# A two-layer graph network on one core: the rarely taken rounds of layer one move out of the loop, and unread products are added to it

## The chip, the core and the metric

The kernel runs on one core of one Trainium2 chip. The core has five engines that run side by side and meet at semaphores: TensorE (PE: matrix products; its weight loads are shown as PEld), VectorE (DVE), ScalarE (ACT), GpSimd (POOL, which here issues the gathering DMAs) and SyncE (SP, which issues the plain DMAs). The metric is the time of one execution on the device in microseconds. The kernel before takes 2933.87 us (median of 3 runs, 2928.56 to 2934.1).

## The reference

There are 6250 nodes with 64 features each and 200000 edges, each with a source, a target and (for layer one) a weight; the edges are sorted by target. Cut to what matters:

```python
h = maximum(layernorm(x), 0)
# layer one
m = edge_weight[:, None] * (h @ W + b)[src]
agg = segment_sum(m, dst) / (segment_sum(edge_weight, dst)[:, None] + 1e-6)
x = x + relu(agg)
h = maximum(layernorm(x), 0)
# layer two
m = gelu(concat(h[src], edge_attr) @ W_msg + b_msg)
agg = segment_sum(m, dst)
x = x + gelu(((1 + eps) * h + agg) @ W_upd + b_upd)
```

## The kernel before, in words

The 200000 edges are cut into 196 groups of 1024 edges, and four groups (numbered s = 0 to 3) make a body, so that both layers have 49 bodies. Since the edges are sorted by target, the targets of a group mostly lie within a window of 72 nodes. A group's sum by target is a product of its edges' rows with a one-hot matrix of target places (`onehots`, L1373; the product is `window`, L989), which VectorE adds to the sums of all nodes (`sums`, L1463, then a small `tick`, L1483).

**Layer one** gets the source rows of a group in two ways. Some tiles of 128 edges (3 or 4 of 8) are gathered by GpSimd from a table. The other tiles (`JA` of them, 5 or 4) are not gathered: VectorE makes one-hot matrices of their sources and targets (`tile_onehots`, L1379 and L1381; all of a group by `build`), TensorE multiplies them into a small adjacency block (`blocks_of`, L927), ScalarE copies the block out (L720), and once per body TensorE multiplies the whole adjacency with the table (`adjacency_sums`, 98 products of L946). That result is copied (L734), turned back (`sums_back`, L957 and L958) and copied by VectorE (`rows_of_sums`, L1420) to stand beside the gathered rows.

The bodies of layer one run in stretches that `STRETCHES` sets: bodies 0 to 13 are a loop (the first stretch, 5 tiles of 5 columns), 14 and 15 stand as straight code, 16 to 46 are a loop again (the second stretch, 4 tiles of 10 columns), and 47 and 48 stand as straight code. In the function `first` one body works one ahead: TensorE makes the blocks of body b + 1 while it sums body b, and VectorE builds the one-hots of groups 2 and 3 of body b + 1 and of groups 0 and 1 of body b + 2. The order on each engine is the order in which `first` is written. A ring of two groups holds the one-hots of the tiles, so `build` of a group waits until TensorE has multiplied the group two before it: `build(ahead, b + 1, 2)` waits for the tiles of `blocks_of(ahead, b + 1, 0)`.

Targets that do not fit a tile's 5 or 10 columns need **further rounds** (`further_rounds`). They stand at the head of every body on TensorE and VectorE: a flag of the body (`more_flags`) is loaded, and a conditional block follows that is passed over where the flag is not set. The block holds a whole round for all tiles: on VectorE a loop with three or four instructions for each of the 16 or 20 tiles, on TensorE all their products. In this execution no body enters it: the trace has no instruction of the lines inside it, such as L1503 or L1522. TensorE's loops in layer one are emitted with a hint for the jump back (`hint_back_edge`), VectorE's without.

**Layer two** (`second`) is another loop over 48 bodies and a straight last one. It picks two of eight tiles by products with the whole table (L917), gathers the others, multiplies the edges' features (L1115) and sums with windows as before.

`busy(n)` issues n products of 192 columns (L1018) into a bank of PSUM that nobody reads. Before the change it stands in the last body of layer one, between the layers and at the end of layer two.

## Time and profile before

| what | value |
|---|---|
| median of 3 runs | 2933.87 us |
| the profiled execution, its own time | 2940.75 us |
| its span, first to last instruction | 2938.9 us |
| TensorE busy / VectorE busy | 89% / 71% |
| granted clock of TensorE over the span | 0.947 |
| layer one's bodies | about 104 to 1350 us |
| layer two's bodies | about 1400 to 2908 us |

The profiled execution took 1.9 us more than its span, and 6.9 us (0.2%) more than the median of the runs. In the rows below, a timeline row gives an instruction's start, its duration, its engine and line, what it writes and reads, and in square brackets how long its engine had been idle before it and who ended that; "issue" means that the engine waited for nothing that the profile shows. Several instructions of one kind in a row are merged into one row with their count.

### The profile page before, as it was taken

How to read it: one execution, taken by the hardware profiler on the slowest of the kernel's cores; microseconds unless marked ns; L12 is line 12 of the kernel's file. 1: busy time of each engine (PE TensorE's matmuls, PEld its weight loads, DVE VectorE, ACT ScalarE, POOL GpSimd, SP SyncE). 2: the span in 40 equal slices, each digit the busy share in tenths (PEclk: the TensorE clock that was granted, in tenths of full speed). 3: DMA queues.
4: the chain of work that ended last, by engine and by line, in shares of the span. 5: the costliest groups of instructions: out<-in, count | busy, mean ns of one | idle time of the engine just before them, and what ended most of it. 6: DMA issues, size and time to landing. Idle time of an engine off the chain costs nothing.

```text
span 2938.9 us, 72786 instructions
## 1 busy us (share of the span) xinstructions
PE 2615.2 (89%) x22325; PEld 2440.5 (83%) x22326; DVE 2088.3 (71%) x4375; ACT 1617.3 (55%) x5144; POOL 1820.8 (62%) x1911
## 2 busy tenths in 40 slices
PE   1788877887888888788999999999999999999999
PEld 1678777777777777777999999999999999999998
DVE  8766667667667666766777777777777777777774
ACT  2555555455555555545556656556656565665653
POOL 3355555555555555552777777777777777777771
PEclk9999998888888888888999999999999999999997
DMA  6010111110111111111454444544444545444442
GB/s 125 16 20 19 21 21 20 22 22 20 21 22 20 21 22 21 20 21 44 109 124 119 121 121 118 121 118 121 117 120 118 123 115 123 119 119 120 118 120 45
DMA packets 473383, 216.56 MB, mean 74 GB/s; under 512 B 264997, under 2 KB 442025, under 8 KB 473077
## 3 DMA queue, kind: packets, MB, share of 16 engines
q1 hardware_dynamic: 412404, 151.55, 19.8%
q0 software_dynamic: 60672, 62.25, 11.5%
q14 instruction: 276, 2.25, 0.3%
q8 instruction: 31, 0.51, 0.1%
HBM read 208.14 MB, written 5.51 MB: 73 GB/s over the span
## 4 chain that ended last, share of the span: by engine, by line
PE 52%; DVE 0%; ACT 0%; issue 0%; DVEq 0%
PE ps L917 38%; PE ps L1115 7%; PE ps L989 4%; PE ps L1104 3%; PE ps L1062 1%; PE ps L1018 0%; DVE rows L1446 0%; DVE parts L1211 0%; DVE sel L1442 0%; DVE room L1635 0%; ACT h_sb L847 0%; DVE h_sb L1666 0%; DVE h_sb L1671 0%; ACT h_sb L865 0%; DVE tick L1483 0%
## 5 line engine op out<-in xcount | busy, mean ns | idle before, releaser
L628 POOL DMA_INDIRECT rows<-p_table,idx x1176 | 1110.0, 944 | 395.5 <-issue 350.0
L917 PE MATMUL ps<-parts,pick_all 128*128 128x448 f32 x5488 | 1167.0, 369 | 2.2 <-DVE parts L1211 2.2
L917 PEld LDWEIGHTS ps<-parts,pick_all 128*128 128x128 f32 x5488 | 1017.8, 188 | 83.5 <-issue 2.6
L628 POOL DMA_INDIRECT rows<-h_table,idx x720 | 694.2, 964 | 616.1 <-ACT room L759 422.5
L720 ACT COPY adj<-ps 128x500 f32<-128x500 f32 (+1 forms) x848 | 394.8, 518 | 308.2 <-PE ps L927 298.0
L927 PE MATMUL ps<-hot_c,hot_p 128*128 128x125 f32 (+1 forms) x2336 | 470.7, 304 | 63.9 <-issue 57.3
L927 PEld LDWEIGHTS ps<-hot_c,hot_p 128*128 128x128 f32 x2336 | 393.0, 212 | 80.5 <-issue 72.2
L1442 DVE TENSOR_TENSOR sel<-ps,mask 128x896 f32<-128x896 f32 x196 | 214.0, 1092 | 310.1 <-PE ps L917 302.0
L1425 DVE TENSOR_SCALAR pick_all<-src_all,node_f 128x1792 fp32r<-128x1792 int16 x196 | 406.6, 2075 | 28.6 <-issue 26.2
L989 PE MATMUL ps<-onehot,room 128*65 128x72 f32 (+1 forms) x3400 | 227.0, 237 | 193.7 <-DVE onehot L1373 98.2
L989 PEld LDWEIGHTS ps<-onehot,room 128*65 128x65 f32 (+1 forms) x3400 | 197.7, 144 | 228.2 <-issue 118.2
L946 PE MATMUL ps<-adj,h_sb 128*64 128x160 f32 (+1 forms) x4802 | 352.7, 312 | 8.9 <-issue 7.9
L1373 DVE TENSOR_TENSOR onehot<-iota,dw 128x360 f32<-128x360 f32 (+1 forms) x196 | 99.4, 507 | 357.8 <-issue 354.2
L946 PEld LDWEIGHTS ps<-adj,h_sb 128*64 128x64 f32 x4802 | 340.8, 152 | 14.8 <-issue 12.4
L1446 DVE TENSOR_REDUCE rows<-sel 128x128 f32<-128x896 f32 x196 | 342.8, 1749 | 6.7
L1381 DVE TENSOR_SCALAR hot_c<-iota_c,scal 128x250 fp32r<-128x250 f32 (+1 forms) x848 | 325.8, 384 | 0.0
L1379 DVE TENSOR_SCALAR hot_p<-iota_p,scal 128x256 fp32r<-128x256 f32 (+1 forms) x848 | 309.6, 365 | 20.8 <-PE ps L927 20.5
L927 PE MATMUL ps<-hot_lo,hot_p 128*128 128x250 f32 x1056 | 285.2, 304 | 0.0
L847 ACT ACTIVATE h_sb<-room 128x512 f32<-128x512 f32 x98 | 62.0, 632 | 356.0 <-DVE room L1635 356.0
L927 PEld LDWEIGHTS ps<-hot_lo,hot_p 128*128 128x128 f32 x1056 | 230.3, 218 | 0.0
L1115 PE MATMUL ps<-W1b_sb,eT 128*128 128x128 f32 x1568 | 216.6, 281 | 0.0
L1381 DVE TENSOR_SCALAR hot_lo<-iota_c,scal 128x250 fp32r<-128x250 f32 x528 | 213.4, 404 | 0.0
(180 smaller groups left out, 2592.4 us busy)
## 6 DMA issues: line engine op xcount, KB each, us to landing
src_all<-keys SPq DMA_DIRECT2D x196, 448.0 KB
ea<-in_edge_attr_dram SPq DMA_DIRECT2D x196, 256.0 KB
rows<-p_table,idx POOLq DMA_INDIRECT x1176
rows<-h_table,idx POOLq DMA_INDIRECT x720
x_sb<-in_x_dram SPq DMA_DIRECT2D x6, 224.0 KB, 4.0
h_table<-h_sb SPq DMA_DIRECT2D x6, 224.0 KB
p_table<-h_sb SPq DMA_DIRECT2D x6, 224.0 KB
out_dram<-h_sb SPq DMA_DIRECT2D x6, 224.0 KB
```

Source lines behind the costliest of these rows:

```text
L628: nc.gpsimd.indirect_dma_start(out=rows[:, s, j, 0:D], out_offset=None, in_=table[:, :], in_offset=bass.IndirectOffsetOnAxis(ap=idx[:, s, ...
L720: nc.scalar.copy(adj[:, :, t * z.WT:(t + 1) * z.WT], psA[t % BANKS1][:, 0:KH * KW * z.WT].rearrange("p (k w) -> p k w", w=z.WT)).then_inc( ...
L917: last = nc.tensor.matmul(to, hot[:, k, t * P:(t + 1) * P], parts[:, part, k, :, :].rearrange("p a d -> p (a d)"), start=(k == 0 and part ...
L927: last = nc.tensor.matmul(to[:, k * KW * z.WT:(k + 1) * KW * z.WT], one[:, k * P:(k + 1) * P], two[i], start=(i == 0), stop=(i == z.WP - 1))
L946: last = nc.tensor.matmul(psX[h:h + D, 0:z.cols], h_sb[:, n, :], adj[:, n, 0:z.cols], start=(n < 2), stop=(n >= NB - 2))
L989: last = nc.tensor.matmul(psW[s % 2][at:at + width, :], lhs(j), hot[:, j, :], start=(j < sets), stop=(j >= n - sets))
L1115: last = nc.tensor.matmul(psM[:, q * P:(q + 1) * P], eT[:, q * P:(q + 1) * P], W1b_sb[:, :], start=True, stop=True)
L1379: nc.vector.tensor_scalar(one, iota_p[:, :], number(0), None, ALU.is_equal)
L1381: last = nc.vector.tensor_scalar(two[i], iota_c[:, 0:KW * z.WT], number(1), number(2 + i), ALU.is_equal, ALU.mult)
L1425: nc.vector.tensor_scalar(pick_all[:, q % 2, :].rearrange("p (k e) -> p k e", k=KA), src_bc[:, q % 2, :, 0:PICKS * P], node_f[:, 0:1], Non ...
L1442: nc.vector.tensor_tensor(sel[:, :, :, :], ps[:, bank:bank + PICKS, 0:NA * D].rearrange("p t (a d) -> p t a d", d=D), of.unsqueeze(3).to_b ...
L1446: nc.vector.tensor_reduce(rows[:, q % SLOTS, J0:J, 0:D], sel[:, :, :, :].rearrange("p t a d -> p t d a"), AX.X, ALU.add).then_inc(s_prow, 1)
```

## The change

Two things change in layer one. First, the further rounds of all bodies stand in one block (`all_rounds`) at the head of the last body, on TensorE and on VectorE. It is entered only where a new flag `row_any` (the maximum of the bodies' flags, one more VectorE instruction before the loops) is set, and then runs over all bodies. The loops and the other straight bodies hold no such block any more. Second, `busy(10, psX[:, 0:IDLE])` stands ahead of each pair of windows, for the 48 bodies that have one after them: two times ten products of 192 columns in each body, written into the bank of the adjacency sums, which the next `adjacency_sums` starts anew.

```diff
+        row_any = sb("row_any", [1, 1], i32)
...
-            def further_rounds(z, b, more):
-
-                with pe.If((more & (1 << SLOTS)) > 0):
+            def further_rounds(z, b):
+
+                with pe.If((more_flags(b) & (1 << SLOTS)) > 0):
                     count = pe.value_load(row_b[0:1, bass.ds(b, 1), 0], min_val=1, max_val=N)
                     before = pe.value_load(row_b[0:1, bass.ds(b, 1), 1], min_val=0, max_val=N * BODIES)
-                    pe.wait_ge(s_sumTc, b + 2)
-                    pe.sem_inc(s_passed, 1)
                     with pe.Fori(0, count) as i:
...
-            def busy(n):
+            def busy(n, to=psG):
 
                 for _ in range(n):
-                    nc.tensor.matmul(psG, idle[:, 0:P], idle[:, 0:IDLE], start=True, stop=True)
+                    nc.tensor.matmul(to, idle[:, 0:P], idle[:, 0:IDLE], start=True, stop=True)
...
+            def all_rounds():
+
+                with pe.If(pe.value_load(row_any[0:1, 0:1], min_val=0, max_val=1) > 0):
+                    pe.wait_ge(s_sumTc, BODIES + 1)
+                    for z in ZONES:
+                        with pe.Fori(z.first, z.end) as b:
+                            further_rounds(z, b)
+
             def first(b, here, ahead, further):
                 more = more_flags(b)
-                further_rounds(here, b, more)
+                if not ahead:
+                    all_rounds()
                 if ahead:
                     blocks_of(ahead, b + 1, 0)
                 sums_back(here, b)
@@
                         blocks_of(ahead, b + 1, s)
                     if s == 1:
                         pe.wait_ge(s_sumc, b + 2)
+                    if ahead:
+                        busy(10, psX[:, 0:IDLE])
                     for r in (s - 1, s):
...
+            meta(nc.vector.tensor_reduce(row_any[:, :], row_r[:, 2, :], AX.X, ALU.max))
...
+            def all_rounds():
+
+                with dve.If(dve.value_load(row_any[0:1, 0:1], min_val=0, max_val=1) > 0):
+                    for z in ZONES:
+                        with dve.Fori(z.first, z.end) as b:
+                            further_rounds(z, b)
...
             def first(b, here, ahead, further):
                 more = more_flags(b)
-                further_rounds(here, b, more)
+                if not ahead:
+                    all_rounds()
                 for s in range(SLOTS):
                     dve.wait_ge(s_dw[0], b * SLOTS + (s + 1))
                     onehots(0, s, s_oh[0], here)
```

VectorE at the head of the second stretch's loop, before: the flag of the body (`row_i`) is loaded, and the conditional jump on line 1487 leads over the block of further rounds, whose first rows these are.

```order
L1451 TENSOR_LOAD row_i
L1451 ISA x2
L1487 REGISTER_ALU
L1487 COMPARE_AND_BRANCH
L1488 ISA
L1488 TENSOR_LOAD row_b
L1488 ISA x2
L1489 ISA
L1489 TENSOR_LOAD row_b
L1489 ISA x2
L1490 UNCONDITIONAL_BRANCH
```

The block ends some 190 rows further down with the jump on line 1487, behind which the one-hots of group 0 stand:

```order
L1490 COMPARE_AND_BRANCH
L1487 UNCONDITIONAL_BRANCH
L1560 REGISTER_ALU
L1373 TENSOR_TENSOR onehot<-iota,dw 128x360
L1387 ISA
L1391 ISA
L1379 TENSOR_SCALAR hot_p<-iota_p,scal 128x256
L1381 TENSOR_SCALAR hot_c<-iota_c,scal 128x250
```

The same place on VectorE now (lines are those of the changed kernel, some 11 to 19 higher):

```order
L1602 ISA
L1462 TENSOR_LOAD row_i
L1462 ISA x2
L1579 REGISTER_ALU
L1384 TENSOR_TENSOR onehot<-iota,dw 128x360
L1398 ISA
L1402 ISA
L1390 TENSOR_SCALAR hot_p<-iota_p,scal 128x256
L1392 TENSOR_SCALAR hot_c<-iota_c,scal 128x250
```

The load of the flag is now followed by the one-hots of group 0 at once. The whole loop has 184 rows where it had 382.

TensorE in the second stretch's loop, ahead of the windows of groups 2 and 3, before (last block of group 3, then the windows):

```order
L927 MATMUL ps<-hot_c,hot_p 128x250
L927 MATMUL ps<-hot_lo,hot_p 128x250
L995 REGISTER_ALU
L989 MATMUL ps<-onehot,room 65x72 x5
L995 REGISTER_ALU
L989 MATMUL ps<-onehot,room 65x72 x5
```

And now:

```order
L928 MATMUL ps<-hot_c,hot_p 128x250
L928 MATMUL ps<-hot_lo,hot_p 128x250
L1017 MATMUL ps<-ident 128x192 x10
L994 REGISTER_ALU
L988 MATMUL ps<-onehot,room 65x72 x5
L994 REGISTER_ALU
L988 MATMUL ps<-onehot,room 65x72 x5
```

Ten products of the identity stand between the last block and the first of the two windows. Nothing is moved on ScalarE, GpSimd or SyncE.

## Rows read from the trace of the kernel before

**Rows 1.** The page: TensorE's granted clock in 40 slices of the span, in tenths

```profile
PEclk9999998888888888888999999999999999999997
```

**Rows 2.** Windows: length, busy PE, PEld, DVE, ACT, POOL; clock, DMA share, GB/s

```profile
104.50:389.00 284.50, 238.21 (x2940) 225.11 (x2941) 183.13 (x714) 160.81 (x637) 151.37 (x157) 0.96 0.10 20
495.00:1288.00 793.00, 640.54 (x6314) 611.20 (x6313) 541.37 (x1829) 408.60 (x1421) 448.48 (x467) 0.87 0.11 21
1375.00:2900.00 1525.00, 1519.01 (x10975) 1396.44 (x10976) 1137.02 (x1191) 917.70 (x2663) 1112.98 (x1177) 0.99 0.48 117
```

**Rows 3.** Waits, 495 to 1288 us: total us, times, longest

```profile
DVE onehot L1373 <- issue: 242.1, 59, 8.2
```

**Rows 4.** Timeline of VectorE, one body of the second stretch

```profile
706.50 0.06 DVE L1483 MEMSET tick<- 1x1 f32 x1
714.12 0.53 DVE L1373 TENSOR_TENSOR onehot<-iota,dw 128x360 f32<-128x360 f32 x1 [7.56 <-issue]
714.57 0.43 DVE L1379 TENSOR_SCALAR hot_p<-iota_p,scal 128x256 fp32r<-128x256 f32 x1
...
728.91 0.52 DVE L1373 TENSOR_TENSOR onehot<-iota,dw 128x360 f32<-128x360 f32 x1
...
733.91 0.06 DVE L1483 MEMSET tick<- 1x1 f32 x1
```

**Rows 5.** Timeline of TensorE, the same body

```profile
703.09 8.65 PE L946 MATMUL ps<-adj,h_sb 128*64 128x160 f32 x98 [0.17 <-issue]
...
716.55 0.27 PE L927 MATMUL ps<-hot_lo,hot_p 128*128 128x250 f32 x1
718.92 0.81 PE L989 MATMUL ps<-onehot,room 128*65 128x72 f32 x10 [2.10 <-DVE room L1420]
720.43 1.17 PE L989 MATMUL ps<-onehot,room 128*65 128x72 f32 x10 [0.70 <-DVE onehot L1373]
...
729.48 0.84 PE L989 MATMUL ps<-onehot,room 128*65 128x72 f32 x10 [2.15 <-DVE onehot L1373]
```

**Rows 6.** Timeline of VectorE at the heads of the straight bodies 14 and 47

```profile
411.22 0.46 DVE L1373 TENSOR_TENSOR onehot<-iota,dw 128x288 f32<-128x288 f32 x1 [3.60 <-issue]
...
1310.02 0.53 DVE L1373 TENSOR_TENSOR onehot<-iota,dw 128x360 f32<-128x360 f32 x1 [2.81 <-issue]
```

**Rows 7.** Timeline of VectorE at the jump back of layer two's loop

```profile
1804.91 2.08 DVE L1425 TENSOR_SCALAR pick_all<-src_all,node_f 128x1792 fp32r<-128x1792 int16 x1 [0.55 <-issue]
```

**Rows 8.** Timeline of VectorE at the heads of bodies 1, 13, 17 and 46

```profile
128.40 0.46 DVE L1373 TENSOR_TENSOR onehot<-iota,dw 128x288 f32<-128x288 f32 x1 [6.47 <-issue]
...
392.34 0.46 DVE L1373 TENSOR_TENSOR onehot<-iota,dw 128x288 f32<-128x288 f32 x1 [6.85 <-issue]
...
495.21 0.53 DVE L1373 TENSOR_TENSOR onehot<-iota,dw 128x360 f32<-128x360 f32 x1 [8.16 <-issue]
...
1287.48 0.53 DVE L1373 TENSOR_TENSOR onehot<-iota,dw 128x360 f32<-128x360 f32 x1 [7.53 <-issue]
```

**Rows 9.** Timeline of TensorE, body 16

```profile
467.14 0.35 PE L927 MATMUL ps<-hot_c,hot_p 128*128 128x250 f32 x1 [3.24 <-issue]
...
483.78 6.98 PE L946 MATMUL ps<-adj,h_sb 128*64 128x160 f32 x98 [0.23 <-issue]
490.93 0.35 PE L927 MATMUL ps<-hot_c,hot_p 128*128 128x250 f32 x1 [0.18 <-issue]
```

**Rows 10.** Timeline of VectorE, body 16

```profile
467.89 0.36 DVE L1379 TENSOR_SCALAR hot_p<-iota_p,scal 128x256 fp32r<-128x256 f32 x1 [4.37 <-PE ps L927]
```

**Rows 11.** Windows, within the body of rows 5 (columns as rows 2)

```profile
704.40:707.80 3.40, 3.40 (x33) 3.40 (x32) 1.93 (x9) 0.60 (x4) 2.49 (x4) 0.60 0.14 29
```

**Rows 12.** TensorE alone (busy, clock, DMA share, GB/s), one body of the first stretch

```profile
185.70:207.50 21.80, 17.98 (x233) 1.00 0.10 20
```

**Rows 13.** Timeline of TensorE between the layers

```profile
1352.74 1.49 PE L1018 MATMUL ps<-ident 128*128 128x192 bf16 x16
1354.07 0.36 PE L1062 MATMUL ps<-W_sb,sums_sb 65*128 65x65 f32 x2
```

More of the change, by code:

```diff
@@ L1483, in sums, with further_rounds @@
                 nc.vector.memset(tick[:, s:s + 1], 0.0).then_inc(s_done, 1)
-            def further_rounds(z, b, more):
-                with dve.If((more & (1 << SLOTS)) > 0):
+            def all_rounds():
[3 more added lines that the diff above has]
+                            further_rounds(z, b)
+            def further_rounds(z, b):
+                with dve.If((more_flags(b) & (1 << SLOTS)) > 0):
                     count = dve.value_load(row_b[0:1, bass.ds(b, 1), 0], min_val=1, max_val=N)
```

## The prediction, made blind

> **What bounds the kernel now.** I began with the page's row of the granted clock: it is lower in the first half of the span than in the second [rows 1]. Split by stage [rows 2], layer two has TensorE busy for 1519.01 of 1525 us at a clock of 0.99: it is bound there, and the change touches nothing in it. Layer one is another case: in the second stretch TensorE is busy for 640.54 of 793 us at a clock of 0.87, VectorE for 541.37. Neither is full, so something makes them take turns.
>
> The list of waits names it: VectorE stood for 242.1 us ahead of the one-hots of line 1373, for nothing that the profile shows [rows 3]. The timeline of one body shows where. VectorE ends a body with the tick at 706.50, and its first instruction of the next starts at 714.12, 7.56 us later [rows 4]. From 714.12 to the tick at 733.91 it hardly pauses, so a body lasts VectorE's 19.8 us and this stall: (1287.48 - 495.21) / 29 turns = 27.32 us [rows 8]. TensorE waits three times for VectorE in such a body, 2.10, 0.70 and 2.15 us [rows 5]. In the first stretch the body is (392.34 - 128.40) / 12 = 22.0 us, with a stall of 6.5 to 6.9 us [rows 8].
>
> In that stall VectorE does two things: it jumps back, and it jumps over the block of further rounds. The straight bodies only have the second jump, and stall for 3.60 and 2.81 us [rows 6]. Layer two's loop only has a jump back, and stalls for 0.55 us [rows 7]. So the skip costs about 3.4 us, and the jump back in layer one costs the rest, about 4.1 us, where the loop is long because the block stands in it. I read both as code that has to be fetched after a far jump.
>
> **The change part by part.**
>
> *The stall on VectorE.* It loses the skip, 3.4 us. What is left is bounded by 4.1 us (the jump back as dear as now) and 0.55 us (as in layer two, whose loop is of a like length now that 382 rows have become 184). I take 0.6 us, and it turns out not to matter, because something else is late next.
>
> *What is late next.* `build` of group 2 of the next body waits for the first tile of `blocks_of(ahead, b + 1, 0)`, which on TensorE stands behind the adjacency sums, and these stand behind the last window, which waits for VectorE's one-hots of group 3. That is a ring through both engines. VectorE's leg, from the start of that build to the end of the one-hots of group 3, is 728.91 + 0.52 - 714.57 = 14.86 us [rows 4]. TensorE's leg is 0.05 us to start (729.48 after 729.43), the last window 0.84 us [rows 5], a gap of 0.23, the adjacency sums 6.98 and a gap of 0.18 us [rows 9], and then 0.75 us from the first block to VectorE's start, 467.14 to 467.89 [rows 9, 10]: 9.03 us. Together the ring takes 23.9 us. Body 16, entered without a jump back, shows this wait already, 4.37 us of it [rows 10].
> VectorE alone would need 733.97 - 714.57 = 19.4 us from that build to its last tick, then the stall and 0.45 us of one-hots: 20.5 us with a stall of 0.6, and 23.95 with 4.1 us. So anything up to 4 us in the stall is hidden behind TensorE's leg.
>
> *The clock in TensorE's leg.* The adjacency sums took 6.98 us in body 16 and 8.65 us in the body of rows 5, where the granted clock was 0.60 from 704.4 to 707.8 [rows 5, 9, 11]: much of that was at the lower of its two levels. That is 1.67 us more in the ring, 25.6 us. Now the clock falls behind each of the idle stretches of rows 5. Afterwards the first (2.10 us, waiting for `rows_of_sums`) is all but gone, since VectorE gets there earlier relative to TensorE: the blocks of groups 0 and 1 and `sums_back` take TensorE 5.1 us from the end of the adjacency sums (711.74 to 716.82), and the copy lets the first window start 718.92 - 714.57 = 4.35 us after the build's start [rows 4, 5], which is then 0.75 us behind those sums, so also 5.1 us after them. The last one, ahead of the last window, stays. TensorE works for 27.32 - 4.95 = 22.4 us in a body now; the clock of 0.87 accounts for 0.13 x 27.32 = 3.6 us of that, which leaves 18.8 us, so in a ring of 23.9 us it would idle for 5.1 us, and for 3.4 us with the new products. Most of that, 2.5 to 3 us, lies ahead of the last window, longer than the 2.15 us after which the clock fell. But an idle stretch of 1.84 us in body 16 left the sums at 6.98 us, and how it falls depends on where the stretch lies. I take half of the bodies with the lower clock: 24.7 us a body. The bounds are 23.9 and 25.6 us.
>
> *The twenty products.* Sixteen of them took from 1352.74 to 1354.07, 0.083 us each [rows 13], so ten take 0.83 us at the full clock and about twice that at the lower. In the second stretch both tens lie where TensorE would wait for one-hots of group 1 and of group 3, so I cost them at nothing; without that cover the second ten would add 0.83 us a body.
> In the first stretch there is no cover. TensorE was busy for 17.98 us in a body of 21.8 us at full clock [rows 12]; with 20 x 0.083 = 1.66 us, and 0.5 us of short gaps around the windows and the sums, a body takes 20.1 us. The ring there is shorter, and VectorE alone needs 22.0 - 6.7 + 0.6 = 15.9 us, so TensorE is full and the products stand on the path. Without them it would be about 18.4 us.
>
> *TensorE's own skip.* In straight code TensorE stalls too, 3.24 us in body 16 ahead of the first block [rows 9]; it lies in the ring. In the loops, which are hinted, the gap is 0.17 us [rows 5]. I take 3.2 us for each of bodies 14, 15, 16 and 47. The last body keeps its skip, now over a longer block: nothing changes. The one extra VectorE instruction for the flag costs some tenths at most.
>
> *Sum, against the profiled execution's 2940.75 us.* Second stretch 29 x (27.32 - 24.7) = 76 us. First stretch 13 x (22.0 - 20.1) = 25 us. Straight bodies 4 x 3.2 = 13 us. Together 114 us, so 2827 us for such an execution. It stood 6.9 us above the median of the runs shown, which is what I forecast: 2933.87 - 114 = 2820 us.
>
> The Trainium skill ("Runtime: NRT & Kernel Launch", section "Instruction fetch mechanics") says that code is held in pages, that what follows in sequence is fetched ahead, and that a taken branch out of the pages held has to wait for its target. By this rule a loop shorter than a page can still lie across the edge of one and pay at its jump back. The stalls of rows 6 and 7 agree with it: far forward jumps pay, layer two's short loop doesn't. By the rule the first two loops may go on paying about 4 us, by the row of layer two 0.6 us; by the sum above both give 2820 us.
>
> **The rivals.**
>
> *The clock stays up (2797 us).* If the shorter idle stretches never lower it, the second stretch takes 23.9 us a body: 29 x 3.42 = 99 us, with 25 and 13 us 137 us. For it: two of the three waits of rows 5 vanish. Against: the one left is as long as any now.
>
> *The clock falls in every ring, and the products are in the way (2845 to 2869 us).* With 25.6 us a body the second stretch gives 29 x 1.72 = 50 us, in all 88 us and 2846 us. If the second ten also delays the last window, 0.83 us a body more, 2870 us. For it: the sums took 8.65 us in the settled second stretch. Against: the cover of 2.5 us or more.
>
> *The skip was not the stall (2921 us).* If the 7.5 us belong to the jump back or to the load of the flag, which both stay, only TensorE's 13 us in the straight bodies is won. Against it are the straight bodies of rows 6, which don't jump back, and layer two's loop, which loads the flag as well and stalls for 0.55 us.
>
> *Layer two's loop pays at its jump back (slower, 2988 us).* All code behind layer one moves to another place. If VectorE's loop of layer two then stalled as the skip does, 3.5 us more on each of 48 turns, with TensorE full and waiting for VectorE's picked rows, that is 168 us against a gain of 114: 2988 us. It decides from 114 / 48 = 2.4 us a turn that reach TensorE. For it: TensorE has no idle time there [rows 2]. Against it: VectorE is busy for 1137 of 1525 us only [rows 2], some of the 3.5 us would be hidden, and the loop is of the same length as now.
> The Trainium skill's rule on pages (the same section) is what makes this rival possible at all; no run here shows such a loop on an edge.
>
> **How the numbers follow.** My forecast, with half of the rings at the lower clock, gets 0.55 (its own range is 2800 to 2840 us); the clock that stays up 0.16; the fallen clock or exposed products 0.18; the skip that was no stall 0.05; layer two's loop 0.06, of which 0.04 is slower in the end. A difference of 0.2% is about what a measurement of this kernel can tell from none. Faster by more than that: 0.92; within it: 0.03; slower: 0.05. The range of eight in ten is 2775 to 2868 us: it takes in the first two clock cases and nearly all of the third, and leaves out the last two.
>
> **What would show it.** In the profile of the changed kernel the stall ahead of the one-hots of group 0 should be near 0.6 us (up to 4 us would be harmless), and VectorE should now wait for TensorE's blocks ahead of the build of group 2, some 2 to 3.5 us a body. The second stretch's bodies should be 23.9 to 25.6 us apart, the first stretch's near 20.1 us with TensorE full. TensorE's wait for `rows_of_sums` should be gone in the second stretch, and its wait ahead of the last window should remain at 2.5 to 3 us. The adjacency sums should take 7.0 us in some bodies and 8.65 us in others. Layer two should be unchanged. Bodies of 27 us, or a layer two that is longer, would prove me wrong.

## The result, and the profile after

The changed kernel takes 2801.22 us (median of 4 runs, 2788.9 to 2810.56), against 2931.22 us for the kernel before on the same chip (median of 4 runs): ratio 0.9554, 95% interval 0.9515 to 0.9594. It is 4.5% faster, 130 us. The forecast was 2820 us with a range of 2775 to 2868. The profiled execution took 2802.29 us, its span is 2800.5 us.

TensorE's granted clock has risen in the slices of layer one [rows 1], which the page shows:

```profile
PEclk9999999999999999989999999999999999999999
```

The windows by stage (length; busy PE, PEld, DVE, ACT, POOL; clock, DMA share, GB/s), first stretch, second stretch and layer two, answer to [rows 2]:

```profile
104.00:380.00 276.00, 269.65 (x3582) 261.70 (x3578) 215.29 (x799) 181.32 (x707) 166.90 (x176) 1.00 0.11 21
460.00:1150.00 690.00, 606.09 (x6697) 572.06 (x6699) 524.73 (x1774) 390.47 (x1376) 457.61 (x451) 0.96 0.11 21
1260.00:2760.00 1500.00, 1498.27 (x10820) 1374.20 (x10821) 1116.35 (x1159) 898.73 (x2615) 1111.11 (x1176) 1.00 0.49 118
```

The first stretch now has TensorE full (269.65 of 276 us), layer two is as full as it was, and the second stretch is still the one where nobody is full. The list of waits of the second stretch (total us, times, longest) says who waits there:

```profile
DVE hot_p L1390 <- PE ps L928: 99.2, 28, 5.6
PE ps L988 <- DVE onehot L1384: 75.0, 29, 2.8
DVE onehot L1384 <- ACT dw L649: 33.0, 28, 1.2
DVE onehot L1384 <- issue: 13.2, 28, 0.5
```

The 242.1 us that VectorE stood ahead of the one-hots [rows 3] are down to 33.0 + 13.2 us. What has come up is a wait in each direction, once per body: VectorE for TensorE's blocks and TensorE for VectorE's last one-hots. This is the ring, the chain of work that goes through VectorE and TensorE and back. The timeline of VectorE shows it over two turns, one at the full clock and one at the lower:

```profile
513.17 0.06 DVE L1494 MEMSET tick<- 1x1 f32 x1
514.41 0.53 DVE L1384 TENSOR_TENSOR onehot<-iota,dw 128x360 f32<-128x360 f32 x1 [1.18 <-ACT dw L649]
517.69 0.35 DVE L1390 TENSOR_SCALAR hot_p<-iota_p,scal 128x256 fp32r<-128x256 f32 x1 [2.75 <-PE ps L928]
...
538.09 0.53 DVE L1384 TENSOR_TENSOR onehot<-iota,dw 128x360 f32<-128x360 f32 x1 [1.18 <-ACT dw L649]
542.59 0.35 DVE L1390 TENSOR_SCALAR hot_p<-iota_p,scal 128x256 fp32r<-128x256 f32 x1 [3.97 <-PE ps L928]
...
563.56 0.53 DVE L1384 TENSOR_TENSOR onehot<-iota,dw 128x360 f32<-128x360 f32 x1 [1.18 <-ACT dw L649]
```

Against [rows 4]: the stall ahead of the one-hots of group 0 is 1.18 us where it was 7.56, and behind them VectorE now waits 2.75 or 3.97 us ahead of `build` of group 2. The profile puts the end of this stall down to ScalarE's `dw`, but in e11 below stalls of one length (0.73 to 0.75 us) are put down to `dw` in some bodies and to `issue` in others, so I count it as a stall and not as a wait for ScalarE. The bodies here are 538.09 - 514.41 = 23.68 and 563.56 - 538.09 = 25.47 us long. TensorE at the end of the second of these bodies, to be held against [rows 5]:

```profile
553.49 1.00 PE L1017 MATMUL ps<-ident 128*128 128x192 bf16 x10
554.32 0.79 PE L988 MATMUL ps<-onehot,room 128*65 128x72 f32 x10
557.88 0.84 PE L988 MATMUL ps<-onehot,room 128*65 128x72 f32 x10 [2.77 <-DVE onehot L1384]
558.91 8.65 PE L947 MATMUL ps<-adj,h_sb 128*64 128x160 f32 x98 [0.18 <-issue]
```

The ten products run and the window of group 2 follows them at once; then 2.77 us idle, and the last window. The other waits of [rows 5], 2.10 and 0.70 us, have gone. After such an idle stretch the granted clock was 0.61 from 558.9 to 562.3 us, as in [rows 11]:

```profile
558.90:562.30 3.40, 3.39 (x32) 3.40 (x34) 3.18 (x13) 0.30 (x2) 2.48 (x4) 0.61 0.16 29
```

That falls on the adjacency sums, here 8.65 us long as in [rows 5]. Not every idle stretch of this kind lowers the clock in time to hurt. Two of the same length, 2.56 us, two bodies apart:

```profile
485.34 0.84 PE L988 MATMUL ps<-onehot,room 128*65 128x72 f32 x10 [2.56 <-DVE onehot L1384]
486.39 6.98 PE L947 MATMUL ps<-adj,h_sb 128*64 128x160 f32 x98 [0.21 <-issue]
...
532.70 1.46 PE L988 MATMUL ps<-onehot,room 128*65 128x72 f32 x10 [2.56 <-DVE onehot L1384]
534.09 7.81 PE L947 MATMUL ps<-adj,h_sb 128*64 128x160 f32 x98
```

Behind the first the window takes 0.84 and the sums 6.98 us, all at the upper of the clock's two levels (granted clock 1.00, which is 2.4 GHz); behind the second the granted clock is 0.50 (1.2 GHz) while the window takes 1.46 us, and 0.76 over the first 3.4 us of the sums, which take 7.81 us.

The bodies follow suit: from body 17 (head at 440.59 us) to body 46 (1152.85) 29 turns take 712.26 us, 24.56 us each. Twelve of them last 23.35 to 23.80 us, the other seventeen 24.9 to 26.4 us, 25.2 on average.

In the first stretch two heads of VectorE, and TensorE's share of the stretch between them (busy, clock, DMA share, GB/s), answer to [rows 8, 12]:

```profile
142.24 0.46 DVE L1384 TENSOR_TENSOR onehot<-iota,dw 128x288 f32<-128x288 f32 x1 [1.20 <-ACT dw L649]
161.00 0.46 DVE L1384 TENSOR_TENSOR onehot<-iota,dw 128x288 f32<-128x288 f32 x1 [1.20 <-ACT dw L649]
```

```profile
142.24:161.00 18.76, 18.46 (x252) 1.00 0.11 21
```

A body takes 18.76 us and TensorE is busy for 18.46 of them. The two places where a skip or a jump back is left, the head of the last body, whose skip is now longer, and the jump back of layer two:

```profile
1199.28 0.53 DVE L1384 TENSOR_TENSOR onehot<-iota,dw 128x360 f32<-128x360 f32 x1 [4.77 <-issue]
...
1706.05 2.08 DVE L1436 TENSOR_SCALAR pick_all<-src_all,node_f 128x1792 fp32r<-128x1792 int16 x1 [0.53 <-issue]
```

The skip in the last body costs VectorE 4.77 us, once, where the shorter one took 3.48 us. TensorE's skip there shows as well, ahead of `sums_back`, before and now:

```profile
1338.96 0.31 PE L957 MATMUL ps<-eye,xs 128*40 128x64 f32 x2 [0.38 <-ACT xs L734]
...
1204.18 0.28 PE L958 MATMUL ps<-eye,xs 128*40 128x64 f32 x2 [3.25 <-issue]
```

TensorE waited 0.38 us for ScalarE before and stands for 3.25 us now. Behind that the granted clock is 0.50 from 1206.4 to 1213.2 us, and the 28 products of `busy` in this body take 4.56 us where they took 2.47. Layer two's jump back costs what it did [rows 7].

Added up by the heads of VectorE's bodies, against the 2938.9 us of before [rows 8]: 5.0 us up to body 1, 38.8 us in the twelve turns to body 13, 10.8 us to body 17, 80.0 us in the 29 turns to body 46; then 2.8 us lost up to the products between the layers (the last body alone is 4.0 us longer: its longer skips and the clock behind them), and 6.6 us less in all that comes after. Together 138.4 us, the difference of the spans.

No run shows these 6.6 us to be the change's doing. From the last pick of layer two to the end the profiled execution of before took 48.9 us, at a low clock:

```profile
2900.00:2920.00 20.00, 18.14 (x141) 17.50 (x139) 7.00 (x12) 3.23 (x6) 0.00 (x0) 0.72 0.06 13
2920.00:2938.90 18.90, 13.89 (x71) 13.38 (x70) 5.25 (x9) 2.31 (x4) 0.00 (x0) 0.50 0.37 73
```

That of the changed kernel took 36.6 us, at 1.00 in the matching 20 us. That is 12.3 us less; 5.7 us of it were lost ahead of that pick, where a body of layer two took 30.91 us instead of 30.81. The same end is short in the profile of e2 (37.3 us), which is the kernel before with the products, and long in those of e5, e6 and e8 (48.5 to 49.4 us), so 12 us there come and go without the change.

### The profile page after: what moved, and what is told of

The parts are those of the page before. It is cut to its first block, busy times and chain, and to the rows that moved or that the text cites. A ratio compares the mean times of both kernels' runs of the same rounds, so it can differ in the third digit from the quotient of the medians.

```text
span 2800.5 us, 74471 instructions
## 1 busy us (share of the span) xinstructions
PE 2598.1 (93%) x23285; PEld 2418.8 (86%) x23286; DVE 2096.8 (75%) x4376; ACT 1611.5 (58%) x5144; POOL 1848.4 (66%) x1911
## 4 chain that ended last, share of the span: by engine, by line
PE 55%; DVE 0%; ACT 0%; issue 0%; DVEq 0%
PE ps L918 40%; PE ps L1125 7%; PE ps L988 4%; PE ps L1114 3%; PE ps L1072 0%; PE ps L1017 0%; DVE rows L1457 0%; DVE parts L1221 0%; DVE sel L1453 0%; DVE room L1654 0%; ACT h_sb L848 0%; DVE h_sb L1685 0%; DVE h_sb L1690 0%; ACT h_sb L866 0%; DVE tick L1494 0%
## 5 line engine op out<-in xcount | busy, mean ns | idle before, releaser
L629 POOL DMA_INDIRECT rows<-h_table,idx x720 | 720.9, 1001 | 451.8 <-ACT room L760 249.1
L928 PE MATMUL ps<-hot_c,hot_p 128*128 128x125 f32 (+1 forms) x2336 | 422.2, 285 | 46.7 <-issue 35.7
L928 PEld LDWEIGHTS ps<-hot_c,hot_p 128*128 128x128 f32 x2336 | 351.4, 193 | 63.7 <-issue 47.7
L947 PE MATMUL ps<-adj,h_sb 128*64 128x160 f32 (+1 forms) x4802 | 328.4, 298 | 4.1 <-issue 3.6
L947 PEld LDWEIGHTS ps<-adj,h_sb 128*64 128x64 f32 x4802 | 312.7, 145 | 13.2 <-issue 5.9
L988 PE MATMUL ps<-onehot,room 128*65 128x72 f32 (+1 forms) x3400 | 213.2, 233 | 90.0 <-DVE onehot L1384 80.5
L988 PEld LDWEIGHTS ps<-onehot,room 128*65 128x65 f32 (+1 forms) x3400 | 188.6, 141 | 114.4 <-DVE onehot L1384 91.7
L928 PE MATMUL ps<-hot_lo,hot_p 128*128 128x250 f32 x1056 | 251.1, 279 | 0.0
L1125 PEld LDWEIGHTS ps<-W1b_sb,eT 128*128 128x128 f32 x1568 | 197.6, 191 | 11.1
L848 ACT ACTIVATE room<-room 128x512 f32<-128x512 f32 x98 | 62.0, 632 | 247.5 <-DVE room L1654 247.5
```

Of the source, the lines that this page charges most:

```text
L629: nc.gpsimd.indirect_dma_start(out=rows[:, s, j, 0:D], out_offset=None, in_=table[:, :], in_offset=bass.IndirectOffsetOnAxis(ap=idx[:, s, ...
L928: last = nc.tensor.matmul(to[:, k * KW * z.WT:(k + 1) * KW * z.WT], one[:, k * P:(k + 1) * P], two[i], start=(i == 0), stop=(i == z.WP - 1))
L947: last = nc.tensor.matmul(psX[h:h + D, 0:z.cols], h_sb[:, n, :], adj[:, n, 0:z.cols], start=(n < 2), stop=(n >= NB - 2))
L988: last = nc.tensor.matmul(psW[s % 2][at:at + width, :], lhs(j), hot[:, j, :], start=(j < sets), stop=(j >= n - sets))
L1125: last = nc.tensor.matmul(psM[:, q * P:(q + 1) * P], eT[:, q * P:(q + 1) * P], W1b_sb[:, :], start=True, stop=True)
```

## The experiments

Ratios are against the kernel before on the same chip. The changed kernel again, e1, e3 and e4 ran on one chip, e2, e5, e6 and e7 on another, e8, e9 and e10 on a third, e11 on a fourth.

**The changed kernel again (a0_again).**

> The changed kernel once more, beside the variants on one chip. Both theories: 0.955 of the kernel before within its interval (0.951 to 0.959), second-stretch bodies between 23.7 and 25.4 us, first-stretch bodies 18.76 us.

2794.02 us, ratio 0.9533 (0.9507 to 0.9558). Its first stretch has bodies of 18.75 us. Those of its second last 24.32 us on average; most lie between 23.7 and 25.4 us as expected, the extremes are 23.38 and 26.46 us. This is the measure for e1, e3 and e4.

**The rounds moved, no products (e1_rounds_only).**

```diff
-                    if ahead:
-                        busy(10, psX[:, 0:IDLE])
```

> Rounds moved, none of the new products. My theory (the shorter ring through both engines gives nearly all of the gain; the products only hold the clock): first stretch near 17.9 to 18.4 us a body (0.4 to 0.9 us less than with products, since TensorE is full there), second stretch 24.5 to 25.5 us with more bodies at the lower clock, so 2795 to 2835 us, at least 80% of the gain. Rival (the products give a good part of it): second stretch stays above 26 us a body, 2850 us or more.

2820.93 us, ratio 0.9617 (0.9591 to 0.9643): the moved rounds alone give 110 us, the products 27 us more. The first stretch's bodies are shorter without the products, 18.11 us over twelve turns, so twenty of them cost 0.65 us there, and the second stretch's are longer, 25.62 us on average (426.57 to 1169.44 us), a little above what I expected. The window over that stretch has the clock at 0.90, where the changed kernel has 0.96:

```profile
500.00:1140.00 640.00, 533.78 (x5460) 494.64 (x5458) 462.14 (x1579) 347.43 (x1225) 413.34 (x401) 0.90 0.11 21
```

TensorE ahead of the last window and behind it, in a body of 26.1 us:

```profile
574.34 1.46 PE L988 MATMUL ps<-onehot,room 128*65 128x72 f32 x10 [3.28 <-DVE onehot L1382]
575.73 9.21 PE L947 MATMUL ps<-adj,h_sb 128*64 128x160 f32 x98
```

It idles for 3.28 us, and then the last window and the sums run slowly, the sums for 9.21 us. The products compute nothing; they hold the clock up, and pay in the stretch where TensorE idles.

**The products alone (e2_products_only).** The kernel before with `busy(10, psX[:, 0:IDLE])` ahead of each pair of windows.

> The kernel before with the twenty products alone; the further rounds stay in every body on both engines. My theory (VectorE's stall of 7.5 us sets the body, TensorE waits anyway): bodies of the second stretch stay at 27.3 us, of the first at 22 us, the granted clock there rises, and the time stays within 0.4% of before, 2920 to 2942 us. Rival (the clock is what the change gains by, the moved block only helps): 2880 us or less.

2930.31 us, ratio 1.0004 (0.9988 to 1.002): no change. The old stall stands, and the new products wait for the same thing as the window did:

```profile
548.55 0.57 DVE L1375 TENSOR_TENSOR onehot<-iota,dw 128x360 f32<-128x360 f32 x1 [7.97 <-issue]
```

```profile
553.36 1.78 PE L1018 MATMUL ps<-ident 128*128 128x192 bf16 x10 [4.00 <-DVE room L1422]
```

The clock does rise, from 0.87 to 0.91 between 500 and 1100 us, and buys nothing: VectorE's 19.8 us and its stall still set the body, 27.5 us on average. What the products are worth depends on who sets the pace.

**The products in the second stretch only (e3_products_second_stretch).**

```diff
-                    if ahead:
+                    if ahead is ZONES[1]:
                         busy(10, psX[:, 0:IDLE])
```

> Rounds moved, products only in bodies whose next one is of the second stretch's kind (15 to 47). My theory: the products are on TensorE's path in the first stretch, so its bodies fall from 18.76 to 17.9 to 18.4 us, 5 to 11 us in all, and the second stretch stays at 24.5 us: 2790 to 2797 us. Rival (the products hold the clock in the first stretch and pay for themselves there): first stretch 18.8 us or more, 2801 us or more.

2782.11 us, ratio 0.9485 (0.9458 to 0.9511). That is 12 us under a0_again and below what I expected; the 0.65 us of e1 on thirteen turns would be 8.5 us. The two intervals overlap by 0.0004, so the sign is likely and the size is not settled by the times; the traces have it, since the first stretch's bodies are back at 17.8 and 18.3 us in turn.

**The products where TensorE idles (e4_products_at_last_window).** Ten ahead of the first pair of windows, thirty ahead of the last window, in the second stretch only.

```diff
-                    if ahead:
+                    if ahead is ZONES[1] and s == 1:
                         busy(10, psX[:, 0:IDLE])
                     for r in (s - 1, s):
...
+                        if ahead is ZONES[1] and r == SLOTS - 1:
+                            busy(30, psX[:, 0:IDLE])
```

> Rounds moved, products only for bodies 15 to 47: ten ahead of the first pair of windows as in the change, and thirty (2.5 us) between the windows of groups 2 and 3 in place of ten ahead of both, that is inside the wait of 2.8 us which is left. My theory (the clock falls behind that wait and costs 1.7 us in the ring): all second-stretch bodies near 23.7 us, the adjacency sums always 7.0 us, granted clock there 1.00, about 25 us less than the variant with ten, so near 2770 us. Rival (the clock falls for another reason, or thirty products delay the last window): bodies of 25 us or more remain, 2795 us or more.

2763.97 us, ratio 0.9433 (0.9406 to 0.946), 30 us under a0_again. Part of that is the first stretch, which has no products here; against e3, which differs only in the products of the second stretch, it is 18 us. TensorE in settled bodies:

```profile
580.67 2.64 PE L1017 MATMUL ps<-ident 128*128 128x192 bf16 x30
584.11 0.84 PE L988 MATMUL ps<-onehot,room 128*65 128x72 f32 x10 [0.80 <-DVE onehot L1386]
```

```profile
560.41 0.84 PE L988 MATMUL ps<-onehot,room 128*65 128x72 f32 x10 [0.81 <-DVE onehot L1386]
561.44 6.98 PE L947 MATMUL ps<-adj,h_sb 128*64 128x160 f32 x98 [0.20 <-issue]
```

The idle stretch ahead of the last window is 0.8 us instead of 2.77, the sums take 6.98 us in every settled body, and 27 bodies in a row take 23.65 to 23.73 us each. That is the ring at the full clock, measured without any admixture.

**One engine's block at a time (e5_vector_block_moved, e6_tensor_block_moved).** The changed kernel with the other engine's block put back at the head of each body: e5 keeps VectorE's move and undoes TensorE's, e6 the reverse. Each way round the two engines would handle a set flag at different places; no flag is set in this data. The edit of e6 (e5 is the same on TensorE):

```diff
-            def all_rounds():
-                with dve.If(dve.value_load(row_any[0:1, 0:1], min_val=0, max_val=1) > 0):
-                    for z in ZONES:
-                        with dve.Fori(z.first, z.end) as b:
-                            further_rounds(z, b)
...
-                if not ahead:
-                    all_rounds()
+                further_rounds(here, b, more)
```

> The changed kernel with TensorE's block of further rounds back at the head of every body (none is ever entered here; entered, this kernel would not work). My theory: VectorE's stall is what counted; only TensorE's skip in the straight bodies comes back, about 3.2 us for each of four, so 10 to 25 us above the changed kernel, 2804 to 2820 us. Rival (TensorE's block in the loop costs in every body once VectorE is faster, since its skip now lies in the ring): 1 us a body or more, 2840 us or more.

> The changed kernel with VectorE's block back at the head of every body (never entered; entered, it would not work), TensorE's moved. My theory: VectorE's stall of 7.5 us is back and with it bodies of 27.3 and 22 us; only the straight bodies gain, 2915 to 2930 us. Rival (TensorE's part of the move carries half or more of the gain): 2870 us or less.

e5 took 2810.41 us, ratio 0.9594 (0.9567 to 0.9621); e6 took 2922.68 us, ratio 0.9949 (0.9923 to 0.9974). Without VectorE's move nearly all of the gain is lost. In e6 the products and the shorter TensorE program are all there, and so is the stall:

```profile
539.97 0.53 DVE L1384 TENSOR_TENSOR onehot<-iota,dw 128x360 f32<-128x360 f32 x1 [7.23 <-issue]
```

In e5 it is 1.2 us. e6's interval lies just below 1, so TensorE's move gives about 0.5% (0.3 to 0.8%) without VectorE's. TensorE's own skip shows where TensorE is full, in the first stretch: 0.78 us ahead of the first block of a body, where the changed kernel has 0.30. The row of e5, and then that of the changed kernel:

```profile
143.16 2.47 PE L928 MATMUL ps<-hot_c,hot_p 128*128 128x125 f32 x20 [0.78 <-issue]
```

```profile
143.48 2.47 PE L928 MATMUL ps<-hot_c,hot_p 128*128 128x125 f32 x20 [0.30 <-issue]
```

A body of the first stretch takes 19.22 us in e5 instead of 18.76, which is 5.5 us in twelve turns, and bodies 13 to 16 take 6.2 us more. What the skip costs over the whole is at the edge of what the runs tell: 0.9594 against the 0.9533 of a0_again on another chip.

**VectorE's code at another place (e7_code_shifted, e8_second_loop_shifted).** A hundred small instructions in a block that is never entered stand ahead of layer one's loops (e7), or behind them and ahead of layer two's (e8). They are jumped over once.

```diff
+            with dve.If(dve.value_load(row_any[0:1, 0:1], min_val=0, max_val=1) > 0):
+                for _ in range(100):
+                    nc.vector.memset(pad[:, :], 0.0)
```

> The changed kernel with a hundred VectorE instructions in a block that is never entered, ahead of layer one's loops, so that all of VectorE's later code lies a hundred instructions further on. Theory A (what a jump costs on VectorE hangs on where its code lies; all three loops now lie across an edge of what is fetched as one): ahead of the one-hots of group 0 the stall grows from 1.2 to about 4 us, and ahead of the first pick of a body in layer two from 0.55 to about 4 us. By the ring (23.9 us against VectorE's 20 us) layer one hides it: bodies stay at 23.7 to 25.4 us. In layer two, by the rival in my prediction, up to 3.5 us a turn reach TensorE, 168 us in all; if VectorE's two groups of lead hide it, nothing. Theory B (only the length of the jump counts): no stall changes anywhere, and the time is that of the changed kernel, near 2797 us.

> The same hundred instructions in a block that is never entered, but ahead of layer two only, so that layer one's loops on VectorE lie as in the changed kernel. Theory A (place counts): the stall ahead of a body's first pick in layer two is about 4 us, in layer one nothing changes; the time is that of the changed kernel plus what of 3.5 us a turn reaches TensorE, between 2797 us (all hidden by VectorE's lead of two groups) and 2965 us (all exposed). Theory B (length counts): 0.55 us as before, near 2797 us.

e7 took 2780.26 us, ratio 0.9496 (0.9459 to 0.9533); e8 2780.16 us, ratio 0.9463 (0.9432 to 0.9493). Neither lost anything. The stall at the jump back of layer one in e7, and of layer two in e8:

```profile
512.64 0.53 DVE L1385 TENSOR_TENSOR onehot<-iota,dw 128x360 f32<-128x360 f32 x1 [1.14 <-ACT dw L650]
```

```profile
1722.47 2.08 DVE L1437 TENSOR_SCALAR pick_all<-src_all,node_f 128x1792 fp32r<-128x1792 int16 x1 [0.55 <-issue]
```

They are what they were (1.18 and 0.53). For loops of this length the place does not matter to the stall at either of the two offsets tried. Both kernels came out 0.4 to 0.7% below a0_again, and the traces say where. A body of layer two takes 30.69 us in both instead of 30.91, which is about 10 us over the layer; and e7's second stretch took 24.01 us a body at a clock of 0.98, so its share of bodies with the lower clock was smaller. What shortens layer two's body is open. It need not be the place of the code: both kernels also declare one more small tile (`pad`). Among the profiles a body of layer two takes 30.81 us in the two kernels without `row_any` (before and e2), 30.91 us in all those with `row_any` alone (leaving out e11), and 30.69 us in the two with `row_any` and `pad`, on whichever chip; no run varies the tiles alone.

**A shorter leg on VectorE (e9_onehots_early, e10_onehots_early_no_products).** If the ring is the limit, a piece of work taken out of it must shorten every body, though VectorE does no less. VectorE makes the one-hots of group 3 right behind those of group 2, ahead of `build` of group 0 of the body after next, a piece of 3.75 us (from 553.56 to 557.31 us in the changed kernel's trace). e9 is e4 with this edit, e10 is e1 with it.

```diff
-                    dve.wait_ge(s_dw[0], b * SLOTS + (s + 1))
-                    onehots(0, s, s_oh[0], here)
+                    for r in {2: (2, 3), 3: ()}.get(s, (s,)):
+                        dve.wait_ge(s_dw[0], b * SLOTS + (r + 1))
+                        onehots(0, r, s_oh[0], here)
```

> The variant with thirty products at the last window, and VectorE makes the one-hots of group 3 right behind those of group 2, ahead of the build of group 0 two bodies on. My theory (a ring through both engines sets the body: 14.9 us of VectorE and 9.0 us of TensorE): VectorE's leg loses a build of 3.6 us, so the ring would take 20.1 us, and VectorE alone (about 20.5 us with its short stall) or TensorE with its products (18.8 + 3.3 us) set the body: 21 to 22.2 us in the second stretch, about 2700 us. Rival (another chain is as long, as ScalarE's copies of the blocks ahead of the adjacency sums): 23 us or more a body, 2745 us or more.

> The same early one-hots with the rounds moved and none of the new products. My theory: TensorE has little idle time left once the ring is 20.1 us, so the clock hardly falls without products either, and without 3.3 us of them on TensorE the bodies take 20.5 to 21.5 us in the second stretch and 17.1 to 17.8 us in the first: 2670 to 2700 us, no slower than with the products. Rival (without products the clock falls and TensorE, now nearly full, pays for it in every body): 22.5 us or more a body, 2720 us or more.

e9 took 2709.9 us, ratio 0.9241 (0.9211 to 0.9271), 54 us less than e4, which ran on another chip. e10 took 2672.88 us, ratio 0.9115 (0.9087 to 0.9143), 148 us less than e1 and 8.9% faster than the kernel before: it beats both kernels. Windows in the second stretch of e9 and then of e10 (that of e9 takes in the next bodies too):

```profile
500.00:1100.00 600.00, 593.11 (x6938) 569.33 (x6934) 493.74 (x1677) 374.80 (x1320) 428.93 (x430) 1.00 0.13 24
```

```profile
500.00:1000.00 500.00, 450.14 (x5154) 424.38 (x5156) 444.05 (x1492) 329.25 (x1163) 360.23 (x378) 1.00 0.13 25
```

Without the products the clock is 1.00 all the same, because the idle stretch ahead of the last window, which let it fall, is no longer there; a body takes 21.14 us (ten turns from 495.38 to 706.80), and the sums follow at full speed. TensorE in such a body:

```profile
570.25 1.47 PE L988 MATMUL ps<-onehot,room 128*65 128x72 f32 x20
572.17 7.00 PE L947 MATMUL ps<-adj,h_sb 128*64 128x160 f32 x98 [0.46 <-ACT adj L721]
```

With forty products in a body, TensorE is full (593.11 of 600 us), a body takes 22.31 us (25 turns from 499.60 to 1057.32), a little above the 21 to 22.2 us that I expected, and the products are now on the path. Between e1 and e4 products were worth 57 us; between e10 and e9 they cost 37 us. What bounds e10 I did not follow up: TensorE is busy for 90% and VectorE for 89% of that window, and VectorE's wait for the blocks is gone.

**Two bodies a turn (e11_two_bodies_a_turn).** VectorE's loops hold two bodies, so that a turn is about as long as before the change but holds no block that is jumped over.

```diff
-                    with dve.Fori(start, end) as b:
-                        first(b, *zones)
+                    with dve.Fori(0, (end - start) // 2) as turn:
+                        first(turn * 2 + start, *zones)
+                        first(turn * 2 + (start + 1), *zones)
+                    if (end - start) % 2:
+                        first(end - 1, *zones)
```

> The changed kernel, but VectorE's loops in layer one hold two bodies a turn (7 and 15 turns, and body 46 once more as straight code), so that the loop is some 350 rows long, about as long as the loop before with its block (382), while nothing in it is jumped over. It tells apart the two halves into which the prediction split the old stall of 7.5 us, skip 3.4 and jump back 4.1 because the loop is long. Theory L (a long loop pays at its jump back, whatever makes it long): every second body of the second stretch starts behind a stall of about 4 us or more ahead of the one-hots of group 0, the others behind one of about 0.5 us. Up to 4 us are hidden behind TensorE's leg, so bodies stay at 23.7 to 25.4 us and the time within 0.5% of the changed kernel's (2794 to 2801 us); should the stall be over 4 us, each turn loses the rest, at most some 3 us, 15 x 3 = 45 us. Theory S (the skip alone made the stall, some 3 us for the jump forward and the rest for what the jump costs in a loop; length counts for nothing): the stall ahead of every second body is 1.2 us as now and of the others less, and the time is the changed kernel's within 0.3%. Body 47's stall of 0.75 us stays in both.

4098.33 us, and the kernel before beside it 4104.77 us: ratio 0.9987 (0.9974 to 0.9999). This chip was another one than those of the earlier runs, and on it the kernel before needed 40% more than on any of them, so the ratio says nothing about the edit. The trace shows what was different. TensorE stopped again and again within its adjacency sums, where it waited for nothing that the profile shows:

```profile
660.18 0.42 PE L947 MATMUL ps<-adj,h_sb 128*64 128x160 f32 x1 [0.98 <-issue]
662.32 0.42 PE L947 MATMUL ps<-adj,h_sb 128*64 128x160 f32 x1 [1.72 <-issue]
663.73 0.43 PE L947 MATMUL ps<-adj,h_sb 128*64 128x160 f32 x1 [0.98 <-issue]
```

TensorE's stops set the pace there, and a saving on VectorE is lost. VectorE's stalls at the heads of four successive bodies can still be read, as they end by themselves:

```profile
667.26 0.53 DVE L1384 TENSOR_TENSOR onehot<-iota,dw 128x360 f32<-128x360 f32 x1 [0.73 <-ACT dw L649]
698.79 0.53 DVE L1384 TENSOR_TENSOR onehot<-iota,dw 128x360 f32<-128x360 f32 x1 [3.66 <-issue]
743.06 0.53 DVE L1384 TENSOR_TENSOR onehot<-iota,dw 128x360 f32<-128x360 f32 x1 [0.74 <-ACT dw L649]
774.29 0.53 DVE L1384 TENSOR_TENSOR onehot<-iota,dw 128x360 f32<-128x360 f32 x1 [3.62 <-issue]
```

Between two bodies of a turn 0.73 us, at the jump back 3.62 to 3.98 us, all through both stretches. A jump back over some 350 rows thus costs about 2.9 us more than going straight on, with nothing skipped; over 184 rows it costs 0.45 us more (1.18). That is theory L: the long loop is what makes its jump back dear. VectorE's stalls were not longer on this chip in general: the skip in the last body cost 4.06 us there, and 4.1 to 4.9 us in the other profiles of kernels with that block. Still, the long loop was tried on this one chip only, and at one place. (Body 47's stall, which both theories left at 0.75 us, was 0.58.)

## Why the prediction came out as it did

**The step that failed: the first stretch's body, 20.1 us.** It is 18.76 us, which makes 38.8 us of gain in twelve turns, where the sum had 25 us for thirteen. The sum took TensorE's 17.98 busy us in the old body as work that stays, and put 1.66 us of products and 0.5 us of gaps on top. But a busy time is not a floor. The new body has 18.46 us busy with the products in it; less 1.66 us, that is 16.8 us for the same work, 1.2 us less than was taken, and 0.30 us of gaps. The rows show where most of the 1.2 us was. A pair of windows in the old body, and in the new one:

```profile
198.81 0.69 PE L989 MATMUL ps<-onehot,room 128*65 128x72 f32 x8 [1.92 <-DVE room L1420]
200.19 0.71 PE L989 MATMUL ps<-onehot,room 128*65 128x72 f32 x8 [0.69 <-DVE onehot L1373]
...
149.78 1.16 PE L988 MATMUL ps<-onehot,room 128*65 128x72 f32 x16
```

Split by idle time the pair shows 1.40 us busy, in one piece 1.16. In general the last product of a group runs on for 0.16 us after the next group could start (this one ends at 150.94, the next starts at 150.78), and that end counts as busy time of its own only where the engine idles behind it. The old body had six such idle stretches, the new one has one; by 0.16 us each I estimate 0.8 of the 1.2 us.

The products cost what the sum had for them, since TensorE is full. That e1 without them takes 18.11 us and not 17.1 is because TensorE then waits: in two of its bodies it is busy for 17.15 of 18.36 and 17.06 of 17.80 us. The failed term alone made the forecast some 17 us too slow.

**The stall, and what it was.** That it is VectorE's, and that most of the gain hangs on it, e6 and e5 show (0.9949 against 0.9594). I split the 7.5 us into 3.4 us for the skip and 4.1 us for the jump back over a long loop. e11 bears the second half out at 3.6 to 4.0 us. But going straight on costs 0.75 us too, and the stalls from which I took both halves each hold it. Above it the skip costs 2.1 to 2.9 us [rows 6] and the long jump back 2.9 to 3.2 us, so by my estimate from these rows a head with both stalls for 5.7 to 6.9 us. The first stretch does, nearly (6.4 to 7.1); of the second stretch's 7.5 us 0.6 us or more are left without a cause. What was left I put at 0.6 us; it was 1.18 us, twice that, in bodies where it is hidden behind TensorE's leg, as the prediction said of anything up to 4 us. e7 and e8 also took away the ground of my rival on layer two: its loop paid 0.53 us at its jump back, and 0.55 us at another place.
The Trainium skill ("Runtime: NRT & Kernel Launch", section "Instruction fetch mechanics") says that a taken branch waits for its target where that lies outside the two pages that an engine holds, of 256 instructions each by its figure. The 1.18 us of the loop of 184 rows agree with it, and so do e7 and e8: by two pages, which I had overlooked, a loop shorter than one fits wherever it lies. The 3.6 us of the loop of 350 rows agree if that loop reaches into a third page, which no run here shows. The skips of [rows 6] agree less readily, since each leads over some 190 rows only and every one of them stalled.

**The ring.** The prediction had 23.9 us at the full clock and 25.6 us where the adjacency sums run slowly. Measured were 23.68 us in the first body shown and 23.70 us in every settled body of e4; where the clock fell the bodies took 25.2 us on average, a little less than forecast, because the clock fell for different parts of the leg. The waits came out as forecast, or longer: VectorE waits 2.5 to 4.4 us for the blocks, once 5.6, and 3.5 on average (2 to 3.5 us were forecast), TensorE 2.6 us on average ahead of the last window (2.5 to 3 us), and the wait for `rows_of_sums` is gone. e9 and e10 show the ring by cutting it: 3.75 us of VectorE's work out of the leg, with none removed, took 54 and 148 us off, the second with the clock's help.

**The clock.** Half of the bodies with the lower clock was a guess; it was seventeen of 29. More bodies were slow than I took, and each cost less, so the mean of 24.56 us against 24.7 us is in part luck; the gain is 80.0 us against 76. e1 shows that without the products it would have been 25.62 us. The prediction had no time for the rounds without the products: they bring 1.1 to 1.3 us a body there (against 24.56 us, and 24.32 us in a0_again), cost 0.65 us in the first stretch, and bring 27 us over the whole.

**The straight bodies.** I took 3.2 us for each of four, 13 us. From the head of body 13 to that of body 17 10.8 us were gained, and from the head of body 46 to the end of layer one 2.8 us were lost: 8 us. Two things were wrong. TensorE's skips ahead of the first block of bodies 14, 15, 16 and 47 (3.40, 2.15, 3.24 and 3.12 us) are gone, but bodies 14, 15 and 47 became shorter by 1.8, 2.1 and 1.8 us only: in 14 and 15 TensorE stands for `issue` at other places as well, 3.94 and 3.46 us before and 2.21, 3.25 and 2.59 us now, with nothing to skip. (Body 16 gained 6.4 us, since it ends with VectorE's jump back.) And the longer skip of the last body I had put at nothing; that body is 4.0 us longer, with TensorE standing for 3.25 us and then at the lower clock.

**The whole.** The sum had 114 us and the trace has 138.4. The first stretch accounts for 19 of the 24 us that were missing (38.8 and 5.0 against 25), the second for 4; the straight bodies take 5 back, and 6.6 us come from behind layer one, mostly from the clock in the last 49 us of the profiled execution of before. By the medians the gain is 130 us and 16 us were missing. The total could not have told my forecast from the rival in which the clock stays up: that one had 2797 us, 4 us from the result, and only the seventeen slow bodies of the trace rule it out.

## What to carry to other kernels

A conditional block that is never entered is not free inside a loop: it costs the jump over it and, by making the loop long, the jump back, a stall of 7.6 us in a body of 27.3 us here, of which 1.2 us were left without the block. Once such a stall is gone, look for the ring through two engines and move the work that is not in the ring behind that which is; here this was worth 148 us on top of the moved rounds, more than the change itself (130 us). Unread products pay only where TensorE idles, sets the pace afterwards, and would otherwise have its clock fall; put them where the idle stretch is, and measure them again after each other change, since their sign turned between e4 and e9.

## What the runs showed of the hardware that was not expected

- The kernel before took 2930 to 2933 us (medians) on three chips and 4105 us on a fourth, with the clock at 0.84 over the span. In e11's profile, the only one from that chip, TensorE stopped for up to 2.4 us within a row of products. What stopped it is open.
- The end of the kernel, from layer two's last pick on, took 36.6 to 37.3 us in ten of the fourteen profiles and 48.5 to 49.4 us in four (before, e5, e6, e8), there with a granted clock of 0.7 and then 0.5. These 12 us are as much as some of the differences between the variants.
- VectorE's stall at a body's head, with nothing skipped, has three sizes: 0.73 to 0.76 us straight on within a stretch, 1.14 to 1.22 us at the jump back of the changed kernel's loops, 3.6 to 4.0 us at that of a loop of about 350 rows.
- The length of an idle stretch does not settle whether the clock falls behind it: after 2.56 us the adjacency sums took 6.98 us at 486.39 and 7.81 us at 534.09. With 0.8 us (e4) they took 6.98 us in every settled body.
